# Second attention's scores on two 64-row tiles of TensorE, with one copy of the keys and exponentials over two PSUM banks

## What is computed

```python
q = proj(hs, Wq, bq, S); k = proj(at, Wk, bk, T); v = proj(at, Wv, bv, T)   # by heads of 32
scores = einsum('bhsd,bhtd->bhst', q, k) / sqrt(32)
scores = clip(scores, -50, 50); scores = where(attend, scores, -10000); scores = clip(scores, -50, 50)
probs = softmax(scores); ctx = einsum('bhst,bhtd->bhsd', probs, v)
delta = layernorm(rs * (ctx @ Wo.T + bo)) * gamma + beta
```

## Time and profile before

| | us |
|---|---|
| median of 3 runs | 472.7 (471.65 to 473.21) |
| the profiled execution's own time | 472.69 |
| its span, first to last instruction | 471.0 |
| PE busy in the span | 443.2 (94%) |
| DVE busy | 316.1 (67%) |
| ACT busy | 244.7 (52%) |
| POOL busy | 111.0 (24%) |

### The profile page before, as it was taken

One profiled execution on the slowest core, in us unless ns is written; L12 is line 12 of the kernel. 1 busy time (PEld: TensorE's weight loads), 2 busy tenths in 40 slices (PEclk: granted clock), 3 DMA queues, 4 the chain that ended last, 5 costly groups with the idle time before them and its releaser, 6 DMA issues.

```text
span 471.0 us, 9958 instructions
## 1 busy us (share of the span) xinstructions
PE 443.2 (94%) x3838; PEld 279.1 (59%) x3847; DVE 316.1 (67%) x573; ACT 244.7 (52%) x370; POOL 111.0 (24%) x126
## 2 busy tenths in 40 slices
PE   8999899999899899999998888899999999999997
PEld 5556565655355345454555667577775565556996
DVE  4995596679867877765755455888867985555111
ACT  4755744764666356464847668477744682221000
POOL 2220400025024000001084364644422251000000
PEclk9999999999999999999999899899999999999999
DMA  8998988934795145333497998766242370000111
GB/s 268 328 376 310 372 292 262 330 93 146 219 295 139 53 109 160 78 91 82 111 306 197 272 316 312 266 214 225 85 135 90 90 221 26 0 0 0 48 51 58
DMA packets 59183, 82.73 MB, mean 176 GB/s; under 512 B 20100, under 2 KB 43652, under 8 KB 57988
## 3 DMA queue, kind: packets, MB, share of 16 engines
q1 hardware_dynamic: 59136, 82.14, 55.2%
q10 hardware_dynamic: 2, 0.01, 0.0%
HBM read 58.76 MB, written 14.42 MB: 155 GB/s over the span
## 4 chain that ended last, share of the span: by engine, by line
PE 68%; DVE 12%; SPq 7%; DMA 4%; issue 4%; ACT 2%; POOL 2%; ACTq 0%; DVEq 0%; POOLq 0%
PE psum L1597 13%; PE psum L208 8%; PE psum L206 8%; PE psum L1647 8%; PE psum L1430 6%; PE psum L673 4%; PE psum L1544 3%; PE psum L1439 3%; PE psum L1497 3%; DMA kst<-k_scratch 2%; SPq L237 2%; PE psum L1373 2%; PE psum L1527 2%; PE psum L1548 2%; DMA w_stage<-in_w 2%
## 5 line engine op out<-in xcount | busy, mean ns | idle before, releaser
L208 PE MATMUL psum<-wv_p,kv_p 128*128 128x512 f16 x288 | 66.1, 379 | 0.5 <-DVE khl L228 0.5
L206 PE MATMUL psum<-kv_p,wk_p 128*128 128x376 f16 x384 | 66.0, 322 | 0.3 <-DVE khl L228 0.3
L1253 ACT ACTIVATE e<-psum,mask_bias 128x448 f32<-128x448 f32 x96 | 53.6, 635 | 20.6 <-PE psum L1527 16.1
L206 PEld LDWEIGHTS psum<-kv_p,wk_p 128*128 128x128 f16 x384 | 37.5, 98 | 24.6 <-issue 0.6
L208 PEld LDWEIGHTS psum<-wv_p,kv_p 128*128 128x128 f16 x288 | 28.0, 98 | 32.8 <-issue 1.0
L1946 DVE TENSOR_SCALAR e<-e 128x1344 f32<-128x1344 f32 x32 | 32.3, 1010 | 11.5 <-ACT e L1253 11.5
L1544 PE MATMUL psum<-e,vst 128*32 128x112 f32 x768 | 34.9, 266 | 3.9 <-issue 3.3
L1597 PE MATMUL psum<-xt,wg_b 128*128 128x448 f16 x176 | 36.9, 352 | 0.3 <-issue 0.3
L1597 PE MATMUL psum<-xt,wu_b 128*128 128x448 f16 x176 | 36.9, 352 | 0.0
L1647 PE MATMUL psum<-h_p,wd_r 128*128 x176 | 36.0, 366 | 0.0
L1647 PEld LDWEIGHTS psum<-h_p,wd_r 128*128 128x128 f32 x176 | 33.1, 188 | 2.7
(11 more groups left out here) (197 smaller groups left out, 853.9 us busy)
## 6 DMA issues: line engine op xcount, KB each, us to landing
kst<-k_scratch SPq DMA_DIRECT2D x32, 384.0 KB, 6.3
kv_raw<-in_ctx_feat SPq DMA_DIRECT2D x12, 768.0 KB, 6.3
w_stage<-in_w SPq DMA_DIRECT2D x6, 1408.0 KB, 8.7
cn<-in_ctx_tok SPq DMA_DIRECT2D x8, 768.0 KB, 9.6
k_scratch<-khl SPq DMA_DIRECT2D x128, 48.0 KB, 2.0
v_scratch<-vsp SPq DMA_DIRECT2D x24, 256.0 KB, 2.8
vst<-v_scratch SPq DMA_DIRECT2D x8, 768.0 KB, 4.6
qst<-qhl SPq DMA_DIRECT2D x32, 112.0 KB, 5.2
```

The lines of the kernel that those rows point to most:

```text
L206: mm = pe.matmul(psum[:, kv_bank(p), 0:TQ], wk_p[:, u, k, n * P:(n + 1) * P], src[:, v, k, 0:TQ], **ends)
L208: mm = pe.matmul(psum[:, kv_bank(p), :], src[:, u, k, n * P:(n + 1) * P], wv_p[:, v, k, :], **ends)
L1253: act.activation(e[g][:, c, :], psum[:, D_S + (TC * g + c) % 4, 0:4 * S], ACT.Exp, bias=mask_bias[:, b, c:c + 1], scale=1.0 / (WS * QS)).t ...
```

## The change

- Keys: `k_scratch` gets the order (batch, row half r, part, feature, group, j), with head hh = 2r + j. `kst` holds each key once: rows 0 to 63 the heads with r = 0, rows 64 to 127 those with r = 1. A batch takes half the bytes, so there are four buffers (`KST`) in the same space, fetched by two DMAs a batch where there were four.
- Scores: m now counts pairs of groups (m = 2b + pair), and a chunk c of a pair is a step of its own: 16 products over 64 rows, alternating between the two row halves, each half into a bank of its own; high and low queries are accumulated (v = 0, 1). Two slots of two banks each take turns, so step c waits for the exponentials two steps back.
- Exponentials: one instruction over both banks, 2 x 448 columns, 48 of them where there were 96. `e` is two buffers of a pair each; `exps(m)` waits for all values of the pair two back, and after a folded batch for all four additions of POOL.
- Clips: one per chunk of a pair, 896 columns, 48 where there were 32; `values` waits chunk by chunk.
- Order: PE runs the scores one pair ahead, DVE's clips stand at other places, SP's fetches are put in another order.

```diff
-        def keys_fetch(sp, b, g):
-
-            sp.dma_start(kst[b % 2][:, g].rearrange("p h t -> p (h t)"),
-                         k_scratch[b, :, :, g].rearrange("u d h (o t) -> (u d) o (h t)", o=1)
-                         .to_broadcast([2 * HD, 2, 4 * TP])).then_inc(kst_loaded[b % 2], 16)
+        def keys_fetch(sp, b, pair):
+
+            gs_of = slice(2 * pair, 2 * pair + 2)
+            sp.dma_start(kst[b % KST][:, gs_of].rearrange("p g j t -> p (g j t)"),
+                         k_scratch[b, :, :, :, gs_of].rearrange("r u d g j t -> (r u d) (g j t)")).then_inc(kst_loaded[b % KST], 16)
...
-            for g in range(G):
-                keys_fetch(sp, 0, g)
-            sp.wait_ge(down_sum, TILES)
-            for g in range(G):
-                keys_fetch(sp, 1, g)
+            for pair in range(2):
+                keys_fetch(sp, 0, pair)
...
+            for pair in range(2):
+                keys_fetch(sp, 1, pair)
             sp.wait_ge(wq_lo, 1)
             queries_stack(sp, 0, 0)
             queries_stack(sp, 0, 1)
             values_fetch(sp, 0, 0)
             values_fetch(sp, 1, 1)
+            sp.wait_ge(down_sum, TILES)
+            for pair in range(2):
+                keys_fetch(sp, 2, pair)
             queries_stack(sp, 1, 0)
+            queries_stack(sp, 1, 1)
+            for pair in range(2):
+                keys_fetch(sp, 3, pair)
...
             def fold(b, g):
-                pool.wait_ge(e_ready, G * b + g + 1)
+                pool.wait_ge(e_ready, TC * 2 * b + TC)
                 after(pool, pv_sum, G * b)
...
             def exps(m):
-                b, g = m // G, m % G
-                after(act, pv_sum, m - 3)
-                if b and g in FOLDED[b - 1]:
-                    act.wait_ge(z_added, 4 * (b - 1) + 2 * g + 2)
+                b, pair = m // 2, m % 2
+                after(act, pv_sum, 2 * (m - 1))
+                if b and pair == 0 and FOLDED[b - 1]:
+                    act.wait_ge(z_added, 4 * b)
                 for c in range(TC):
                     act.wait_ge(s_sum, TC * m + c + 1)
-                    act.activation(e[g][:, c, :], psum[:, D_S + (TC * g + c) % 4, 0:4 * S], ACT.Exp,
+                    bank = D_S + 2 * ((TC * m + c) % 2)
+                    act.activation(e[pair][:, c], psum[:, bank:bank + 2, 0:4 * S], ACT.Exp,
                                    bias=mask_bias[:, b, c:c + 1], scale=1.0 / (WS * QS)).then_inc(e_raw, 1)
...
             query_hi(1, 0)
             query_hi(1, 1)
+            query_hi(1, 2)
             exps(0)
-            query_hi(1, 2)
-            exps(1)
             query_hi(1, 3)
...
+            def scores(m, c):
+                b, pair = m // 2, m % 2
...
+                after(pe, e_raw, TC * m + c - 1)
+                for i in range(4):
+                    g, j = 2 * pair + i // 2, i % 2
+                    for v in range(2):
+                        for r in range(2):
+                            rows = slice(64 * r, 64 * r + 64)
+                            mm = pe.matmul(psum[:, D_S + 2 * ((TC * m + c) % 2) + r, i * S:(i + 1) * S],
+                                           kst[b % KST][rows, g, j, c * P:(c + 1) * P],
+                                           qst[b // 4][rows, j, v, g, b % 4 * S:(b % 4 + 1) * S], start=v == 0, stop=v == 1)
+                mm.then_inc(s_sum, 1)
...
-            scores(0)
+            scores(0, 0)
+            scores(0, 1)
             query(1, 2)
-            scores(1)
+            scores(0, 2)
             query(1, 3)
             for b in range(B):
                 if b >= 4:
                     project(pe, b - 4)
                     spread(b - 1)
                 if b >= 5:
                     normalized_turn(pe, b - 5)
-                for g in range(G):
-                    m = G * b + g + 2
-                    if m < G * B:
-                        scores(m)
-                    if g == 0 and 1 <= b < 4:
+                for pair in range(2):
+                    m = 2 * b + pair + 1
+                    if m < 2 * B:
+                        scores(m, 0)
+                        scores(m, 1)
+                    values(b, 2 * pair)
+                    if m < 2 * B:
+                        scores(m, 2)
+                    if pair == 0 and 1 <= b < 4:
                         spread(b - 1)
-                    if (b, g) == (B - 1, G - 1):
+                    if (b, pair) == (B - 1, 1):
                         project(pe, 4)
-                    values(b, g)
+                    values(b, 2 * pair + 1)
...
                 if b:
                     invert(b - 1)
-                if b:
-                    clip(G * b + 1)
+                clip(2 * b + 1, 0)
                 if b >= 3:
                     context_low(dve, b - 3)
+                clip(2 * b + 1, 1)
                 if b:
                     normalize(b - 1)
+                clip(2 * b + 1, 2)
                 if b >= 4:
                     delta_variance(dve, b - 4)
+                clip(2 * b + 2, 0)
                 if b >= 5:
                     turned_low(dve, b - 5)
-                clip(G * b + 2)
+                clip(2 * b + 2, 1)
                 if b >= 4:
                     x3_statistics(dve, b - 4)
-                clip(G * b + 3)
+                clip(2 * b + 2, 2)
                 if b >= 4:
                     x3_shift(dve, b - 4)
                 if b == 3:
                     dve.wait_ge(wo_hi, 1)
...
-                if b + 1 < B:
-                    clip(G * b + 4)
```

More of the change, by code:

```diff
@@ L511, in build @@
         wq_p = [at("wq_p0", [P, KC, D], F16, 79104), at("wq_p1", [P, KC, D], F16, 161344)]
-        qst = [at(f"qst{n}", [P, 4, G, HALF], F16, 94464 + n * 14336) for n in range(2)]
+        qst = [at(f"qst{n}", [P, 2, 2, G, HALF], F16, 94464 + n * 14336) for n in range(2)]
         C_BUFS = 3
@@ L559, in queries_stack, with e_head, e_group @@
                 for hh in range(4):
-                    sp.dma_start(qst[n][64 * u:64 * u + 64, hh, gs_of].rearrange("p g s -> p (g s)"),
+                    at_row = 64 * (hh // 2) + 32 * u
+                    sp.dma_start(qst[n][at_row:at_row + 32, hh % 2, :, gs_of].rearrange("p v g s -> p v (g s)"),
                                  qhl[n][32 * hh:32 * hh + 32, :, gs_of].rearrange("d v g s -> d v (g s)")).then_inc(q_stacked[n][pair], 16)
-        e = [at(f"e{r}", [P, TC, 4 * S], F32, 56576 + r * 5376) for r in range(4)]
+        e = [at(f"e{r}", [P, TC, 2, 4 * S], F32, 56576 + r * 10752) for r in range(2)]
+        def e_head(g, c, hh):
+            lo = (g % 2 * 2 + hh % 2) * S
+            return e[g // 2][:, c, hh // 2, lo:lo + S]
+        def e_group(g, c, rows):
+            return e[g // 2][0:rows, c, :, g % 2 * 2 * S:(g % 2 + 1) * 2 * S]
         rz = at("rz", [P, S], F32, 78080)
@@ L902, in _ @@
             values_fetch(sp, 1, 1)
+            sp.wait_ge(down_sum, TILES)
+            for pair in range(2):
+                keys_fetch(sp, 2, pair)
             queries_stack(sp, 1, 0)
+            queries_stack(sp, 1, 1)
+            for pair in range(2):
+                keys_fetch(sp, 3, pair)
             for b in range(B):
-                for g in range(G if b + 2 < B else 0):
-                    sp.wait_ge(s_sum, TC * (G * b + g + 1))
-                    keys_fetch(sp, b + 2, g)
-                if b == 0:
-                    queries_stack(sp, 1, 1)
+                for pair in range(2 if b + KST < B else 0):
+                    sp.wait_ge(s_sum, TC * (2 * b + pair + 1))
+                    keys_fetch(sp, b + KST, pair)
                 if b + 2 < B:
@@ L1276, in _ @@
                     turned_high(act, b - 5)
-                for g in range(G):
-                    m = G * b + g + 2
-                    if m < G * B:
+                for m in (2 * b + 1, 2 * b + 2):
+                    if m < 2 * B:
                         exps(m)
@@ L1514, in _ @@
             query(0, 3)
-            def scores(m):
-                b, g = m // G, m % G
-                if g == 0:
-                    pe.wait_ge(kst_loaded[b % 2], 16 * G * (b // 2 + 1))
-                if b % 4 == 0 and g % 2 == 0:
-                    pe.wait_ge(q_stacked[b // 4][g // 2], STACK)
-                if m == 0:
-                    pe.wait_ge(c_lo, ALL_PARTS)
-                for c in range(TC):
-                    after(pe, e_raw, TC * m + c - 3)
-                    for hh in range(4):
-                        mm = pe.matmul(psum[:, D_S + (TC * g + c) % 4, hh * S:(hh + 1) * S], kst[b % 2][:, g, hh, c * P:(c + 1) * P],
-                                       qst[b // 4][:, hh, g, b % 4 * S:(b % 4 + 1) * S], start=True, stop=True)
-                    mm.then_inc(s_sum, 1)
+            def scores(m, c):
+                b, pair = m // 2, m % 2
+                if c == 0:
+                    if pair == 0:
+                        pe.wait_ge(kst_loaded[b % KST], 32 * (b // KST + 1))
+                    if b % 4 == 0:
```

(22 more changed lines are left out.)

24 lines of the change are left out of this document (12 added, 12 removed).

## The result

The changed kernel takes 510.86 us (median of 4, 503.06 to 515.61), the kernel before beside it 472.95 (471.65 to 477.91): a ratio of 1.0714, with a 95% interval of 1.0643 to 1.0786. The ratio compares fast executions alone, for the changed kernel 510.22 and 503.06 us, since its other two (511.5 and 515.61) were in the chip's slower state. The profiled execution took 510.22 with a span of 508.5, 37.5 longer than before.

What follows compares the result with a forecast made beforehand. PE, nearly gapless, was taken to bound the dense batches. Terms +2.7, -1.9, +5.2 and +19.6 sum to 25.6 on top of 472.7, giving 498.3; with 6 for the clock 504 us, range 488 to 516 (0.78).

Steps and rivals of the forecast that it cites:

- the ring: Batches 4 to 7: DVE waits for PE, PE for DVE, DVE again for PE; batch 17.3 us, before 12.17.
- batch 0: Loop start: third query's copy ahead of the first exponential, third chunk waits some 3 us, folds follow: +2.7 us.
- batches 1 and 2: Folded batches: 11.6 us each where 12.55 before, PE's DMA waits hidden in idle time: -1.9 us for both.
- batch 3 to the spread of batch 4: Weight split now behind a clip that needs the last fold, so project and spread come later: +5.2 us.
- dense stretch, and the clock: Batches 4 to 7: +19.6 us from the order; slower TensorE clock after idle stretches in the loop: +6 us.
- Ahead of the values: Dense batches: PE idles 3.1 us before the first values, until DVE's normalize, queued behind waiting clips, ends.
- Ahead of the spread: Dense batches: PE, done with project, idles another 2.1 us before the spread, until DVE's invert.
- Rival 1: Scores on PE: row tiles take turns, +0.8 us a batch, +6 in all, 510 us; chance 0.07 beyond the range.
- The weight split: DVE in batch 3: split takes 2.3 to 3.2 us behind clip(8, 2), and project(0) waits for it.
- Rival 3: Batches 1 to 3: DMAs were the bound, half the keys' bytes removes PE's waits, 464 us; chance 0.04.
- Rival 4: PE's stream: 768 more instructions bring more waits inside it, +4 us at most; no chance given.
- Rival 2: Dense batches: normalize is done in time, only one wait shows, batch near 14.2 us, time 486; chance 0.08.

Runs made afterwards that it cites:

- e1: Changed kernel with DVE's normalize right behind invert, ahead of the first clip, from batch 4 on: 493.71 us.
- e2: Changed kernel with the first two chunks' scores ahead of project and spread, their exponentials ahead on ACT, from batch 4 on: 495.08 us.
- e3: Changed kernel without row tiles: full-height products, each key twice, same order of all engines: 504.37 us.
- e7: Changed kernel with mended order on PE, ACT and DVE, exps(0) ahead of the third query's copy, no folds: 482.3 us, ratio 1.023.
- e10: Kernel of e9 with normalize ahead of context_low and the second clip in batches 4 to 7: 487.04 us.
- e4: Changed kernel with all eight products of one row half, then all of the other, in each chunk: 512.96 us.
- e6: Changed kernel without folds on POOL, all softmax sums through PE: 508.5 us.
- e11: Kernel of e6 with fetches of keys (batches 4 to 7) and values (2 to 7) cut to 16 columns: 502.64 us.
- e8: Kernel before the change, without folds on POOL: 479.63 us, ratio 1.0164.
- e9: Kernel of e7 with the folds on POOL kept: 484.03 us, ratio 1.0231.

## Why the prediction came out as it did

The forecast was 504.0 (488 to 516); the time is 510.86. Its main reason, the ring in the order of a dense batch, is shown by e1 and e2, and e3 shows that the row tiles and the single keys have no part in that loss. With the order mended, 3.3 (e7) and 2.2 us (e10) of the 24.2 are left, in which the wide exponentials and the split clips may have a part; no run took these out. Against the profiled execution of before:

| term | forecast | measured |
|---|---|---|
| to first scores | 0 | +1.7 |
| batch 0 (first scores to 265.25 before, 274.43 after) | +2.7 | +7.5 |
| batches 1 and 2 | -1.9 | +0.3 |
| batch 3 to the spread of batch 4 | +5.2 | +3.2 |
| dense stretch, and the clock | +19.6, +6 | +24.2 |
| rest | 0 | +0.7 |

That the sum came within 7 us is in part luck: the terms are 9.4 us too low in four places and 3.4 too high in two.

- *Ahead of the values.* 3.1 us of idle time forecast, 3.14 measured, for the reason given.
- *Ahead of the spread.* 2.1 forecast, 0.58 to 1.48 measured. PE came later itself, since the work behind the first wait ran at the lower clock: batch 6, with 0.82, has 14.98 us of PE work where e1 has 12.59. Idle time became slow work, so the order and the clock are one sum, 25.6 forecast if all of the clock's 6 were here, 24.2 measured (e1's comparison puts 6.3 of them on the clock). So the split was off: PE's idle time in the dense stretch rose by 16.3 us (1.3 to 17.7), where I had 19.6, and its busy time by 7.9 (48.1 to 55.9), where I had 6.
- *Scores.* 0.40 a chunk forecast, 0.45 measured (0.89 for two, 327.98 to 328.87), and 0.45 with full height (e3). I had rounded 0.68 / 12 = 0.057 down to 0.05; eight times 0.057 is 0.45. Rival 1 falls: e4 shows what turns cost, some 0.12 a chunk rather than 0.4. The rule of the Trainium skill, "TensorE: Matmul & The Clock Gate", section "LDWEIGHTS (loading the stationary operand)", by which a load of 128 columns would be an estimated 0.107 us, is near what the trace records for a single load, 0.101 on average. It does not price a string of them: the 768 loads together keep PE's loading busy for 21.7 us, 0.028 each, since their records overlap, and 32 loads and products fit into 0.89.
- *Exponentials.* 1.0 forecast, 1.006 measured. *Clips.* 0.53 forecast, 0.55 start to start (320.96 to 321.51).
- *Batch 0* is the step that was mis-sized. The wait of 3.05 came as forecast. Left out of its chain were the query behind it at 1.2 GHz (4.13 us, where the one before takes 2.44; clock 0.50), and a wait of 3.24 inside a string of scores, which stood in batch 1 before (2.27).
- *Batches 1 and 2* gave nothing back. The third chunk waits 2.54 for its exponential, as laid out, but each batch took 12.4 to 12.9, not 11.6; the clock is below 1.00 there too, and how much of the 1.1 that is stays open.
- *The weight split* was there (project(0) follows its end by 0.1 us), at its lower price, 2.28.
- *Rival 3, the DMAs.* With half the keys' bytes, fetched further ahead, the DMA share of batch 1 is 0.56 where it was 1.00 in batches 1 and 2, and these batches gained nothing: their third chunk waits for an exponential that POOL's folds hold up, and without folds (e6) stops inside strings take that place. But its mechanism can count: with POOL out of the way, e11 has batches 0 to 3 shorter by 5.4 us than e6, by fewer bytes (one execution each). *Rival 4* likewise: e6 and e8 show the price of a stop, 1.4 to 2.7 us each. That more products bring more of them is not shown.
- *Rival 2* is e1, which does what that rival described: 493.7, where I had put 486 for it without the clock.

No version that I ran is faster than the kernel before. Mended, the changed layout is level with it in the dense batches' scores on PE (full-height and half-height ones cost the same) and 2 to 3% behind in time: 2.2 to 3.3 us in the dense batches, the rest in batches 0 to 3 and in the scattered first part.

## What to carry to other kernels

When an in-order engine's queue is rewritten, follow the first instruction that now waits for something of this round, and ask who waits for those behind it: moving one 0.6 us instruction out from behind such a wait was worth 16.9 us here. Price each idle stretch of PE twice, for its length and for the slower products behind it (10.6 and 6.3 us in e1's comparison). Work moved off PE's stream can pay although PE has time, and the same move costs where another engine then waits for it: in the profiled executions of batches 0 to 3 the folds save 6.5 us in one order and cost 4.3 in another, and in the medians they save 7 in the first and make no difference in the second. Look, too, at what an instruction will run beside once it is moved: in e10 the clip that came to stand beside POOL's work took twice as long.

## What the runs showed of the hardware

- Half-height f16 products on alternating row halves (and banks) run at 0.028 us each, 0.036 with neighbours on the same half; 16 full-height ones take as long as 32 half-height ones.
- In batches 0 to 3, strings of products stop for 1.4 to 3.2 us where the profile shows no event. With the DMA share down from 0.45 to 0.07 batch 1's stop went (e6 and e11, one execution each); the cause is not shown.
- POOL's folds take 1.13 us an addition now; before, 1.21 and 1.77. DVE's clips mostly no longer run beside them; that this is the cause was not tried.
- A clip of 896 columns that runs beside a POOL addition takes 1.36 us (four times in e10) or 1.44 (at 289.03 in the changed kernel, beside a fold of 1.14); the same clip takes 0.62 in e9, where it does not.
